# Zeroing the expert regions in two halves from 128 partitions, and routing the last batch between chunks of the shared expert

## The reference, cut to what matters

```python
router_logits = x @ gate_w.T                      # 64 experts
probs = softmax(router_logits); topk_w, topk_idx = top_k(probs, 6)
topk_w = topk_w / sum(topk_w)
h = silu(einsum('th,eih->tei', x, experts_w1))    # inner width 176
y = einsum('tei,ehi->teh', h, experts_w2)
routed_out = einsum('teh,te->th', y, combine)     # combine: topk_w at topk_idx
g, u = split(x @ shared_gate_up.T, 2)             # shared expert, inner width 352
return routed_out + (silu(g) * u) @ shared_down.T
```

## Time and profile before

| | us |
|---|---|
| time, median of 3 runs (lowest and highest) | 1508.82 (1508.76 to 1510.72) |
| the profiled execution, its own time | 1508.29 |
| its span in the profile | 1506.3 |
| PE busy | 1278.5 (85% of the span) |
| DVE busy | 827.3 (55%) |
| ACT busy | 462.4 (31%) |
| POOL busy | 379.2 (25%) |
| attention's first score maximum, and the last of the batch rows' residual adds | 82.9 and 673.6 |
| experts' first multiplication, last store issued | 817.7, about 1068 |

### The profile page before, as it was taken

The page is one execution under the profiler, slowest core; times in us unless marked ns, Lnnn a source line. Parts: engine busy times, 40 slices in busy tenths (PEclk is TensorE's granted clock), DMA queues, the critical chain, the costliest instruction groups (busy, mean ns, idle before and its releaser), DMA issues.

```text
span 1506.3 us, 19485 instructions
## 1 busy us (share of the span) xinstructions
PE 1278.5 (85%) x6002; PEld 817.1 (54%) x6002; DVE 827.3 (55%) x2097; ACT 462.4 (31%) x1038; POOL 379.2 (25%) x464
## 2 busy tenths in 40 slices
PE   5599999889989998989703999999346889899988
PEld 4255656556655555554502888888223545456464
DVE  1566856875688567854400333333237677766541
ACT  0255535452545254522000111111013252332411
POOL 0033013361326132620024000000446336150200
PEclk9799999999999999999955999999767899999999
DMA  9999999999999999999974777777321102010000
GB/s 317 196 190 191 191 190 191 189 226 198 191 191 216 209 190 191 208 216 191 191 200 135 233 232 224 229 225 228 103 67 49 42 22 64 20 37 15 1 15 14
DMA packets 206810, 234.39 MB, mean 156 GB/s; under 512 B 12528, under 2 KB 193424, under 8 KB 206352
## 3 DMA queue, kind: packets, MB, share of 16 engines
q1 hardware_dynamic: 180112, 191.50, 58.7%
q0 software_dynamic: 9216, 25.18, 5.4%
q10 hardware_dynamic: 17408, 16.78, 3.3%
HBM read 66.70 MB, written 166.72 MB: 155 GB/s over the span
## 4 chain that ended last, share of the span: by engine, by line
SPq 52%; PE 35%; DVE 7%; issue 4%; POOL 1%; DMA 1%; another core or an unknown queue 0%; ACT 0%; ACTq 0%; POOLq 0%; DVEq 0%
SPq L1980 45%; PE bank L1211 7%; PE bank L1222 7%; SPq L258 3%; SPq L1983 3%; PE bank L1435 3%; PE bank L1446 3%; PE bank L1429 2%; PE bank L1480 2%; PE bank L1590 2%; PE bank L1201 2%; DVE x L1141 2%; PE bank L1540 2%; DVE r L1763 2%; PE bank L1573 1%
## 5 line engine op out<-in xcount | busy, mean ns | idle before, releaser
L692 ACT ACTIVATE r<-bank,negmax 128x128 f32<-128x128 f32 (+3 forms) x256 | 135.2, 528 | 174.2 <-DVE negmax L828 161.1
L532 PE MATMUL bank<-r 128*128 128x512 f32 (+3 forms) x512 | 184.2, 443 | 0.0
L828 DVE TENSOR_REDUCE negmax<-bank 128x1 f32<-128x128 f32 (+3 forms) x256 | 124.5, 487 | 53.3 <-PE bank L533 51.7
L1123 POOL DMA_INDIRECT sent<-r,slots x96 | 95.8, 998 | 178.7 <-DMA sent<-zeros 122.9
L541 PE MATMUL bank<-tables,r 128*128 128x128 f32 x640 | 118.2, 285 | 18.1 <-DVE r L839 16.8
L1278 DVE COPY r<-bank 128x512 f32<-128x512 f32 x64 | 44.3, 692 | 162.1 <-PE bank L1201 162.1
L923 POOL TENSOR_TENSOR r<-r,tables 128x256 f32<-128x256 f32 x56 | 42.3, 755 | 345.6 <-ACT r L675 345.1
L1259 ACT ACTIVATE r<-bank 88x512 f32<-88x512 f32 x64 | 38.0, 594 | 296.3 <-PE bank L1211 296.3
L1211 PE MATMUL bank<-r 128*88 128x256 f32 x512 | 122.9, 383 | 1.3 <-DMA w2buf<-w2T_dram 1.3
L1131 POOL DMA_INDIRECT w2buf<-sent,slots x48 | 49.0, 1021 | 281.1 <-ACTq L1267 259.4
L1222 PE MATMUL bank<-w2buf,r 88*128 88x256 f32 x512 | 118.5, 379 | 0.0
(11 more groups left out here) (253 smaller groups left out, 2333.8 us busy)
## 6 DMA issues: line engine op xcount, KB each, us to landing
sent<-zeros SPq DMA_DIRECT2D x16, 8192.0 KB, 94.1
r<-sent SPq DMA_DIRECT2D x64, 256.0 KB, 3.2
sent<-r ACTq DMA_DIRECT2D x64, 256.0 KB, 3.1
r<-w1T_dram SPq DMA_DIRECT2D x64, 176.0 KB
w2buf<-w2T_dram SPq DMA_DIRECT2D x64, 176.0 KB
r<-w_o_dram SPq DMA_DIRECT2D x1, 2048.0 KB, 14.0
x<-x_dram SPq DMA_DIRECT2D x1, 2048.0 KB, 19.5
out_dram<-x SPq DMA_DIRECT2D x4, 512.0 KB, 2.9
```

The costliest lines, as they stand in the source:

```text
L532: nc.tensor.matmul(at[:, 0:n], QT[g % 2][:, h, i * P:(i + 1) * P], KT[:, 0:n], start=True, stop=False)
L692: nc.scalar.activation(prob[:, u % 4, 0:(i + 1) * P], bank[SCORE[u % 4]][:, 0:(i + 1) * P], ACT.Exp, bias=negmax[:, u:u + 1], scale=1.0, a ...
L828: nc.vector.tensor_reduce(negmax[:, u:u + 1], bank[SCORE[u % 4]][:, 0:(i + 1) * P], axis=AX.X, op=ALU.max, negate=True).then_inc(A["max"], 1)
L1123: nc.gpsimd.indirect_dma_start(sent[:, :], bass.IndirectOffsetOnAxis(ap=slots[:, t, k:k + 1], axis=0), xn1[:, n // TOPK, :], None).then_in ...
```

## The change: two halves, wide slots, and the rest of the last batch behind the experts

1. **Regions.** `sent` now has a lower half with 1,024 rows for each expert (`UPPER` = 65,536 rows in all), then 1,024 rows between, then an upper half with 1,024 rows for each expert. A token copy whose rank in its expert is over 1,024 goes to the upper half. That costs two small DVE instructions for each batch (`upper`) and two on one column in `tile_places`.
2. **Zeroing.** Each half is cleared by 4 DMAs of 16,384 KB, and the rows between by one of 1,024 KB behind the first four. Each DMA now reads 128 partitions and moves runs of 4 KB (1,024 columns), where it was 64 partitions and 1 KB. On the DRAM side neighbouring partitions are 512 KB apart, where neighbouring experts were 2 MB apart. The sends of batches 0 and 1 wait for the lower half and the rows between, those of batches 2 and 3 for the upper half. The zero tile is 128x1024 and lies in `gath1`; the routing's small tiles get a tensor of their own (`scratch`), and `comb` moves to r2.
3. **Slots.** Routing steps move: transposes on PE from slots 1 and 4 to 3 and 6, logits 7 to 9, counts 6 to 7; on DVE `top` 9 to 10, `relative` 10 to 11, `select` 11 to 12 and 13 (two tiles each), `chosen` 13 to 14, `running` 7 to 8 and 9, `ranks` 8 to 10, then `upper` 11, `downward` 12 (two instructions that stood in `ranks` and `nearest`), `nearest` 13, `places` 14, `shares` 15; `portions` goes to slot 8 of group 2, and the six `weigh` to slots 10, 12 and 14 of groups 2 and 3.
4. **Last batch.** Its two row transposes go to banks 6 and 7 with no wait between; the logits come after the three chunks of batch 0, of which one stands behind the transposes; the counts follow one chunk of batch 1, not three. The third chunk of batch 3, its silu and product, `shared_down(3)`, `shared_add(3)` and the six `weigh` go behind the experts; `shared_down(3)` uses banks 6 and 7.

```diff
-SPAN = TOKENS
-FAR = EXPERTS * SPAN
+SPAN = TOKENS // 2
+UPPER = EXPERTS * SPAN
+FAR = 2 * UPPER + SPAN
...
-        zeros = sb("zeros", [P, DIM])
+        scratch = sb("scratch", [P, 1172])
         gath1 = sb("gath1", [P, TOPK, DIM])
+        zeros = gath1[:].rearrange("p k c -> p (k c)")[:, 0:4 * DIM]
...
-                    if at == 7:
+                    if at == 9:
                         route_logits(pe, c, 6)
-                if g % GROUPS == 1 and at == 6:
+                if g % GROUPS == 1 and at == 7:
...
-                if hg == 1 and at in (13, 14, 15):
-                    route.weigh(c, at - 13)
-                if hg == 2 and at in (1, 2, 3):
-                    route.weigh(c, at + 2)
+                if hg >= 2 and at in (10, 12, 14):
+                    route.weigh(c, 3 * (hg - 2) + (at - 10) // 2)
...
+            def upper(self, c):
+                self.step(nc.vector.tensor_scalar(taken, key, 1.0 * SPAN, 1.0 * UPPER, ALU.is_gt, ALU.mult))
+                self.step(nc.vector.tensor_tensor(key, key, taken, ALU.add))
...
-            pool.wait_ge(zeroed[c], 16 * ZERO_PARTS + (16 if c == BATCH - 1 else 0))
+            h = (c + 1) * SEQ > SPAN
+            pool.wait_ge(zeroed[h], 16 * ZERO_PARTS + (16 if h == 0 else 0))
...
-                need(pe, M["sacc"], TB * b + i - 1)
+                if b == BATCH - 1 and i < 2:
+                    pe.wait_ge(R["trips"], 1)
+                else:
+                    need(pe, M["sacc"], TB * b + i - 1)
...
-            for b in range(BATCH):
+            part = UPPER * DIM // P // ZERO_PARTS
+            for h, first in enumerate((0, UPPER + SPAN)):
+                half = sent[first:first + UPPER, :].rearrange("(q r) c -> q (r c)", q=P)
                 for n in range(ZERO_PARTS):
-                    lo = b * SEQ + n * part
-                    sp.dma_start(per_expert[:, lo:lo + part, :],
-                                 zeros[0:EXPERTS].unsqueeze(1).to_broadcast([EXPERTS, part, DIM]))\
-                        .then_inc(zeroed[b], 16)
+                    sp.dma_start(half[:, n * part:(n + 1) * part].rearrange("q (s k) -> q s k", k=4 * DIM),
+                                 zeros.unsqueeze(1).to_broadcast([P, part // (4 * DIM), 4 * DIM]))\
+                        .then_inc(zeroed[h], 16)
...
             route.chosen(c)
-            shared_hidden(dve, 1)
-            route.running(c, 6)
+            shared_hidden(dve, 1, (0,))
+            route.running(c, 6, (0, 1, 2, 3))
             route.ranks(c, 6)
+            route.upper(c)
+            route.downward(c)
             route.nearest(c)
             route.places(c)
+            shared_hidden(dve, 1, (1, 2))
             shared_add(dve, 0)
...
-            shared_hidden(dve, 3)
-            shared_add(dve, 2)
+            experts_vector(dve)
             for k in range(TOPK):
                 route.weigh(c, k)
+            shared_hidden(dve, 3, (2,))
+            return_vector(dve, 0)
             shared_add(dve, 3)
-            experts_vector(dve)
-            for i in range(TB):
+            for i in range(1, TB):
                 return_vector(dve, i)
...
-            shared_up(pe, 0)
-            norm_tensor(pe, N1, c, xn1, 0)
-            pe.wait_ge(N1.done["row"], KC * c + 1)
-            norm_tensor(pe, N1, c, xn1, 1)
+            shared_up(pe, 0, (0, 1))
+            norm_tensor(pe, N1, c, xn1, 0, 6)
+            norm_tensor(pe, N1, c, xn1, 1, 7)
+            shared_up(pe, 0, (2,))
             route_logits(pe, c, 6)
-            shared_up(pe, 1)
+            shared_up(pe, 1, (0,))
             pe.wait_ge(R["lgs"], BATCH)
             route_counts(pe, c, 6)
+            shared_up(pe, 1, (1, 2))
...
-            shared_up(pe, 3)
+            shared_up(pe, 3, (0, 1))
             shared_down(pe, 2)
+            experts_tensor(pe)
+            shared_up(pe, 3, (2,))
             shared_down(pe, 3)
-            experts_tensor(pe)
```

More of the change, by code:

```diff
@@ L964, in build @@
         ZERO_PARTS = 4
-        zeroed = [sem(f"m_zeroed{b}") for b in range(BATCH)]
+        zeroed = [sem(f"m_zeroed{h}") for h in range(2)]
         MCREDIT = ("tr", "trc", "up", "hid", "down", "ey")
@@ L1031, in chosen, with running @@
                 self.dve.wait_ge(R["mask"], c + 1)
-            def running(self, c, at):
-                self.dve.wait_ge(R["count"], c + 1)
-                if c:
-                    self.step(nc.vector.tensor_copy(before[:, 0, :], before[:, TB, :]))
-                for i in range(TB):
+            def running(self, c, at, tiles):
+                if tiles[0] == 0:
+                    self.dve.wait_ge(R["count"], c + 1)
+                    if c:
+                        self.step(nc.vector.tensor_copy(before[:, 0, :], before[:, TB, :]))
+                for i in tiles:
                     n = (TB + i) * EXPERTS
@@ L1300, in experts_vector, with shared_up @@
             step(last_it, False)
-        SGATE, SUP, SDOWN = (0, 2), (1, 3), (4, 5)
-        def shared_up(pe, b):
-            if b == 0:
+        SGATE, SUP = (0, 2), (1, 3)
+        SDOWN = ((4, 5), (4, 5), (4, 5), (6, 7))
+        def shared_up(pe, b, chunks):
+            if b == 0 and chunks[0] == 0:
                 pe.wait_ge(A["exp"], NU * GROUPS * BATCH)
-            for c, (lo, w) in enumerate(SH_CHUNKS):
+            for c in chunks:
+                lo, w = SH_CHUNKS[c]
                 n = 3 * b + c
@@ L2001, in _ @@
                 pool.sem_inc(s, 16)
-            nc.gpsimd.memset(zeros[:], 0.0).then_inc(consts, 1)
+            nc.gpsimd.memset(zeros, 0.0).then_inc(consts, 1)
             nc.gpsimd.memset(ones[:], 1.0).then_inc(consts, 1)
```

116 lines of the change are left out of this document (68 added, 48 removed).

## The result

| | before | after |
|---|---|---|
| time, median (lowest and highest, runs) | 1508.79 us (1507.55 to 1510.72, 4) | 1442.53 us (1441.85 to 1443.59, 4) |
| ratio after to before | | 0.9561, 95% interval 0.9546 to 0.9577 |
| span of the profiled execution | 1506.3 us | 1441.7 us |
| first shared chunk; first expert multiplication; loop's last DVE copy | 673.36; 817.74; 1068.38 us | 675.32; 753.73; 1003.99 us |

66 us faster. It is also outside the 1414 to 1436 that the forecast gave itself together with rival (d), and inside rival (a)'s 1436 to 1450, though for another reason than (a)'s. That the range holds it is luck.

The account below looks back on a forecast made before the run. Zeroing was taken to bind only at the last batch's first send, PE and DVE bounding elsewhere. 1508.3 - 81.2 (earlier experts) - 2.0 (clock) + 0 (behind experts) + 1.5 (attention) = 1426.6, predicted time 1426, range 1401 to 1443 us.

Parts of the forecast that it names:

- rival (d): At the experts' start: PE's or DVE's list runs over, +3 to +6, 1431 us; forecast together with it 60%.
- rival (a): In the attention: DVE's additions in wide slots cost full price and delay PE's run-ahead, +13, 1436 to 1450 us; 12%.
- The zeroing: Zeroing DMAs from 128 partitions in 4 KB runs: 365 GB/s, ending at 407 us, so no send waits for zeros.
- Rival (c): The change doesn't speed the zeroing: 182 GB/s, POOL waits 118 us before its query rotations, time 1598 us; 5%.
- The attention: Moved routing slots: per batch -3.9 in group 1, +1.5 group 2, +2.3 group 3, +0.5 for `top`; three batches +1.5 us.
- The last batch up to the sends: After the attention: slots at 695.5 instead of 702.96 us, 24 sends taking 29.13 us from first to last start.
- PE ... to 731.7, before its first row transpose can start: PE's list before the experts: seven chunks, three downs and two small transposes end at 731.7, transpose possible from 732.3.
- DVE ... 733.9: DVE's list before the experts: `shared_add(2)` ends at 732.3, `shares` and `portions` (1.5) at 733.9, then the first copy.
- The sends' own cost: At the experts' start: first row load 4.62 us after the last send's start, first multiplication 5.8 us after that load.
- The clock: At the experts' first turns: PE works up to them, so they run at full clock, 2.0 us gained.
- Behind the experts: Moved chunk, down and weighings after the loop: covered by the gather's idle time, zero change.
- Rival (b): The attention gets faster: steps leave slots where PE is short, and the 3.26 us gap goes with zeroing traffic; 1407 us; 23%.

Follow-up runs that it names:

- e6: Changed kernel with the routing steps from `running` to `places` moved together into slots 8 to 11, the rest following, on chip A: 1438.6 us, ratio 0.9530.
- r1: The changed kernel again, unaltered, on chip A: 1441.9 us, ratio 0.9550 to the kernel before.
- e5: Changed kernel with POOL waiting after every four of the last batch's sends until they have landed (five pauses), on chip A: 1434.1 us, ratio 0.9502.
- e4: Changed kernel with tile table and loop counts ahead of the waiting chunk products, shared down 2 and all shared batch 3 behind the experts, chip C: 1419.5 us, ratio 0.9453.
- e13: Changed kernel with POOL pausing after every six last-batch sends, and every three following the units in the third and fourth batch's attention, chip D: 1413.1 us, ratio 0.9408.
- e3b: Changed kernel with a small POOL memset behind each last-batch send, and the upper half zeroed in two other forms, chip B: 1443.2 us, one run.
- e12: Changed kernel with the last batch's 24 sends replaced by 24 indirect loads of as many rows, without a pause, chip B: 1442.3 us, one run.
- e8: Changed kernel with the last batch routed and its shared work done in the order of the kernel before, chip B: 1460.5 us, ratio 0.9674.
- r2: The kernel before again, unaltered, on chip A: 1507.7 us.
- e7: Order of e4, with POOL pauses after every six last-batch sends and every one to three in the attention, chip B: 1453.6 us, ratio 0.9636.
- e2: Changed kernel with POOL waiting after every four of the last batch's sends until they have landed, on chip C: 1417.1 us.

## Why the prediction came out as it did

**The zeroing: right in its effect, too low in its size.** Forecast 365 GB/s (337 to 393) and an end at 407; measured 409 and about 380. The window 776 to 778 that I took from below mixed loads and a short store; nothing in the trace of before bounded the store alone. It cost nothing, since no send waits for zeros at either rate. Rival (c) is refuted. The half rate of 64 partitions that the Trainium skill (SBUF — State Buffer, section on the DMA port swizzle) states is in the runs: 202 against 409 at equal runs; its 328 GB/s for 128 partitions is a figure for 1 MB, and these DMAs move 16 MB. The 207 GB/s that its page DMA: Bandwidth & Descriptors gives for 512 KB between partitions was a copy's figure, and a store alone at that distance ran at 409. (The page's 214 is for a distance of 4 MB padded by 4 KB, where the prediction says only "padded".)

**The attention: right as a sum, wrong in two terms that cancel.** Forecast +1.5 for three batches, measured +2.0 (675.32 against 673.36). Group 0 took 0.4 (0.5 forecast), group 1 gave 4.2 to 4.5 (3.9 forecast). Group 2 took 3.9 to 4.2, its upper bound, where I chose 1.5: next to nothing hid DVE's 4.75 us in its wide slots. Group 3 took nothing in two batches and 1.8 in the last (2.3 forecast). In all three its first 15 slots grew by 1.7 to 1.8: the weighings in slots 10 and 14 cost 1.4 us each, that in slot 12 fell into the gap there (the slot takes 4.0 us, 4.8 before), and slots 4 and 5 together changed by 0.4. What follows slot 15 took the growth up where another batch came behind it. That the two errors cancel is luck. e6 shows no more than 3.2 us between the two choices of places (1438.6 against r1's 1441.9), with overlapping intervals.

**The last batch up to the sends: right.** Slots 21.7 us after the first chunk (22.1), sends 29.1 from first to last start.

**"PE ... to 731.7, before its first row transpose can start", "DVE ... 733.9", and rival (d): this is the step that failed.** I summed both lists from durations and let them run through; rival (d) allowed them 3 to 6 us over. They ran over by 15.3, as two products of DVE started 6 and 16 us after PE's matmuls for them were over. e5 shows the cause as far as POOL: on one chip, breaking the run of sends removes both waits and 9.9 of the 77.8 us. Where signals are on time the list runs as I summed it: in e5 `portions` ends DVE's list 59.4 us after the first chunk (60.5 forecast: 733.9 - 673.4), although five pauses lie in it. The sends' own cost was right too: in e4 from the last send's start to the first multiplication 9.8 us (4.6 + 5.8 forecast).

**The clock: wrong, by most of its 2 us.** I expected the first turns at full clock, since PE works up to the experts. In the changed kernel it starts them at 753.73 with 3.55 us, in a window 753 to 757 with a granted clock of 0.57 (1.2 GHz for most of it). It had worked from 733.46 on, after 15.5 us of idling, and the clock was full again from 737 to 753; then it idled 3.0 us for DVE's copy. In e13, where PE's list runs through, it idles 4.0 us for its rows, and the first multiplication takes 3.71. But the same idling does not always end so: e3b and e12 have the same 3.0 us in front of it, and the first multiplication takes 2.78 and 1.96, at a granted clock of 0.69 and 1.00 (753 to 757). In these two the clock had come back to full some us later, at 0.94 and 0.78 from 737 to 741. In e8, with 1.1 us of idling in front of it, it takes 1.96. Of the nine traces with this order of PE's list only e12 has the full clock that I forecast, and e3b part of it. What decides that stays open.

**Behind the experts: zero forecast, zero found.** 437.7 against 437.9 us. On chip A it is 441.1 in r1 against 437.1 in r2, a difference that lies within the 5.1 us over which r1's four runs spread, so zero is known to some 4 us only.

Summed up: +0.5 in the attention, +15.3 between the first chunk and the experts (78.4 against 63.1), +2.0 for the clock and -0.6 from there to the end of the span (688.0 against 688.6) make the 17.1 us by which the span misses the forecast (64.6 less than before, where 81.7 were forecast).

**Rival (b)** asked if the gap of 3.26 us would vanish with the zeroing's traffic. It did not: slot 12 of group 3 takes 3.96 us in the changed kernel with no zeroing on the DMA engines, and 2.82 in e7 with the sends paused. By all that the runs show, the gap was the same lateness as the one that cost the 15 us, in sight before the change: it shrinks with pauses on a late chip (e7) and is as small without them on a quiet one (e4, 2.82). The trace of before also has it among its waits, as time that ended on no instruction:

```profile
ACT r L704 <- remote: 9.8, 3, 3.3
```

I saw the gap, asked only about traffic, and didn't ask what the same POOL work would do to lists with 3 us of slack.

**What stays open.** Why signals were late on chips A and B and in the first comparison, and not on C and D, whether that belongs to the chip for good or to the hour, why one batch of r1 was spared, and what holds them. The changed kernel itself was not run on a quiet chip, nor e13 on a late one; its gain over the changed kernel there is an estimate: r1 and e13 differ by 30 us of span, of which 5.8 lie in the attention, 12.6 between chunk and expert multiplication, and 12.7 behind the loop, but pauses and chip are mixed in that. T3 was not tried by itself. But ACT's silu of chunk 8 starts 10.6 us after PE's matmuls with no wait for DVE left, and a port between DVE and POOL does not explain that. DVE's instructions of one shape also last the same in the run of sends (0.69 for a product) as outside it.

## What to carry to other kernels

A rate that binds at one place is worth what the next limit there leaves, and that was read rightly from the single POOL wait for zeros. When work is moved beside a long run of indirect DMAs of POOL, look in the trace for waits on PE that end long after its matmuls, or on nothing: they are the price of lists that depend on each other with little slack, and a wait of POOL for its own DMAs every four to six, which leaves it 1.7 us without issuing, may be cheaper than the run. Such a pause must not stand where other traffic delays the landing, and kernels are to be compared on one chip: before differed by 7 us between chips, one and the same paused kernel by 17 (e2 1417.1, e5 1434.1).

## What the runs showed of the hardware that I had not expected

- On two chips and in the first comparison instructions of ACT and DVE that waited for PE started 2 to 16 us after its matmuls were over, while POOL issued 24 indirect DMAs without a pause (1.27 us each): with stores and with loads, with a small memset between them, and with waits that POOL passed at once. With a wait until all had landed after every four or six of them (e5, e7) no product of that stretch waited over 3.1 us. On two other chips there was none of it.
- Zeroing stores from SBUF to HBM: 191 and 202 GB/s from 64 partitions, 348 and 409 from 128, in runs of 1 and 4 KB.
- POOL's wait for its last send to land was 1.7 us on quiet DMA engines, and 6.1 behind the zeroing.
